# Second accumulator for early maximum units, values through the query/key banks

## What is computed

```python
b, n, _ = x.shape                       # x: layer-normalised, 4 x 1024 x 256, 16 heads of 16
qkv = x @ Wqkv.T + bqkv
q, k, v = ...                           # by head
scores = einsum('bhqd,bhkd->bhqk', q, k) / 4
attn = softmax(scores)
out = einsum('bhqk,bhkd->bhqd', attn, v) -> b, n, 256
return out @ Wo.T + bo
```

## Time and profile before

| | us |
|---|---|
| median of 3 runs | 1923.58 |
| lowest, highest | 1921.22, 1930.8 |
| the profiled execution's own time | 1933.64 |
| its span, first to last instruction | 1931.9 |
| PE busy | 1852.8 (96%) |
| DVE busy | 1354.6 (70%) |
| ACT busy | 1173.1 (61%) |
| the query, key and value phase, first to last product | 635.3 to 769.7 |

### The profile page before, as it was taken

How to read it: one execution, slowest core, us unless ns; L and a number is a source line. 1 busy time by engine, 2 the same in 40 slices (tenths; PEclk the granted TensorE clock), 3 DMA queues, 4 the chain that set the end, 5 groups by cost and what they waited for, 6 DMA issues and landing times. The chain is left out here.

```text
span 1931.9 us, 51788 instructions
## 1 busy us (share of the span) xinstructions
PE 1852.8 (96%) x19838; PEld 1431.7 (74%) x19838; DVE 1354.6 (70%) x2718; ACT 1173.1 (61%) x2355; POOL 432.4 (22%) x509
## 2 busy tenths in 40 slices
PE   7999899999999887999999999999999999999997
PEld 5788789999999644555555555565546789999997
DVE  7566678444436777899999999999944877444445
ACT  4222544444445543898899989989895644445443
POOL 4122001555542322000000000000000002555541
PEclk9999999999999999999999999999999999999999
DMA  7000211222226565321212111111005311222228
GB/s 306 1 1 1 79 45 35 72 77 78 76 68 200 140 171 144 80 52 47 52 47 47 41 42 42 41 42 42 3 3 200 103 36 35 77 75 78 76 68 267
DMA packets 86539, 149.13 MB, mean 77 GB/s; under 512 B 35620, under 2 KB 69284, under 8 KB 80612
## 3 DMA queue, kind: packets, MB, share of 16 engines
q1 hardware_dynamic: 68428, 103.24, 17.8%
q0 software_dynamic: 17856, 42.60, 8.0%
q10 hardware_dynamic: 24, 0.02, 0.0%
HBM read 96.68 MB, written 48.76 MB: 75 GB/s over the span
## 5 line engine op out<-in xcount | busy, mean ns | idle before, releaser
L2212 ACT ACTIVATE att_scores_pt<-att_scores_psE 128x512 f32<-128x512 f32 x1024 | 598.0, 597 | 69.0 <-PE att_scores_psE L1716 26.9
L1731 DVE TENSOR_REDUCE att_mx<-att_scores_psS 128x1 f32<-128x1024 f32 x472 | 577.9, 1224 | 50.1 <-PE att_scores_psS L1716 18.9
L1716 PE MATMUL att_scores_psE<-att_qs,att_ks 99*32 99x512 bf16 x4096 | 437.3, 382 | 4.0 <-DVE att_scores_psO L2242 3.2
L2314 PE MATMUL att_scores_psO<-att_scores_pt,att_va 128*17 128x256 f32 x4096 | 330.4, 379 | 2.9 <-ACT att_scores_osb L2217 1.3
L1716 PE MATMUL att_scores_psS<-att_ks,att_qs 96*32 96x512 bf16 x3776 | 308.4, 380 | 0.1
L1716 PEld LDWEIGHTS att_scores_psE<-att_qs,att_ks 99*32 99x32 bf16 x4096 | 136.0, 95 | 104.0 <-ACT att_scores_pt L2212 8.5
L658 DVE TENSOR_TENSOR moe_hidT_rest<-moe_ps,moe_hidT_high 128x384 fp32r<-128x384 f32 x142 | 79.1, 557 | 184.5 <-ACT moe_hidT_high L377 167.6
L2314 PEld LDWEIGHTS att_scores_psO<-att_scores_pt,att_va 128*17 128x17 f32 x4096 | 131.5, 98 | 103.3 <-issue 13.2
L865 PE MATMUL moe_ps<-W_rest,moe_srcT_high 128*128 (+2 forms) x824 | 200.6, 325 | 0.0
L283 POOL DMA_INDIRECT expert_rows<-work,moe_slots_i x142 | 140.0, 986 | 218.7 <-ACT work L399 101.3
L1716 PEld LDWEIGHTS att_scores_psS<-att_ks,att_qs 96*32 96x32 bf16 x3776 | 126.0, 97 | 78.1 <-issue 1.6
(11 more groups left out here) (325 smaller groups left out, 3154.0 us busy)
## 6 DMA issues: line engine op xcount, KB each, us to landing
W_gate_up<-in_gate_up_dram SPq DMA_DIRECT2D x2, 6346.0 KB, 22.3
work<-expert_rows SPq DMA_DIRECT2D x12, 1024.0 KB, 7.6
query_key_parts<-att_qkv_parts SPq DMA_DIRECT2D x64, 192.0 KB, 3.0
normalised_rows<-work SPq DMA_DIRECT2D x64, 128.0 KB, 1.9
att_qs<-query_key_parts SPq DMA_DIRECT2D x16, 384.0 KB, 4.4
att_ks<-query_key_parts SPq DMA_DIRECT2D x16, 384.0 KB, 4.5
W_down<-in_down_a_dram SPq DMA_DIRECT2D x2, 2304.0 KB, 28.0
work<-normalised_rows SPq DMA_DIRECT2D x36, 128.0 KB, 2.1
```

The costliest lines, as they stand in the source:

```text
L1716: last = nc.tensor.matmul(out[j:j + 32, :], stationary[:, j:j + 32], moving, start=True, stop=True, tile_position=(0, j), skip_group_check ...
L1731: return nc.vector.tensor_reduce(a.mx[g % 2][:, v:v + 1], bank[:, :, :].rearrange("p h k -> p (h k)"), AX.X, ALU.max)
L2212: nc.scalar.activation(pt[s % 2][:, r, :], psE[use % E_BANKS][:, :], ACT.Exp, scale=HD ** -0.5).then_inc(p_ready, 1)
L2314: last = nc.tensor.matmul(psO[32 * r:32 * r + VC, cols], va[g][:, kt, r * VC:(r + 1) * VC], pt[s % 2][:, r, cols], start=(kt == 0 and part ...
```

## The change

Four things are changed in `qkv_phase`.

- psS becomes two buffers of two banks. Units are counted through both groups (n), unit n goes to psS[n % 2] and waits for the reduction of unit n - 2.
- The banks for that come from psV, which now is psQ: value groups 0 and 1 wait for the rests of m = 2 and m = 3, groups 2 and 3 for the copies of 0 and 1, and the next chunk's m = 0 and 1 for the copies of 2 and 3.
- The values are copied to SBUF by ACT (`values_out`), without a bias. The four copies stand at the end of the chunk in ACT's order. DVE loses the four additions, and its xT_rest subtractions come before the second value step instead of the fourth.
- The bias of the values goes into bo, once: it is loaded as two columns, DVE spreads it over 128 columns (Bvb), PE multiplies it with Wo into psB, a part of psS[0], between value groups 1 and 2 of chunk 2, and DVE adds psB to bo.

```diff
-        ps = [ctx.enter_context(nc.psum_tensor(f"{tag}_ps{i}", [P, 512], F32)) for i in range(6)]
-        psT, psQ, psV = ps[0:2], ps[2:4], ps[4:6]
-        psS = ctx.enter_context(nc.psum_tensor(f"{tag}_psS", [P, 2, HALF], F32))
+        ps = [ctx.enter_context(nc.psum_tensor(f"{tag}_ps{i}", [P, 512], F32)) for i in range(4)]
+        psT, psQ, psV = ps[0:2], ps[2:4], ps[2:4]
+        psS = [ctx.enter_context(nc.psum_tensor(f"{tag}_psS{u}", [P, 2, HALF], F32)) for u in range(2)]
+        psB = psS[0][:, 0, 0:D]
...
-            return early[first:first + PER] if c >= BESIDE else []
+            return list(enumerate(early))[first:first + PER] if c >= BESIDE else []
...
+            def values_out(c, j):
+                act.wait_ge(v_done, c * CT + j + 1)
+                nc.scalar.copy(vt[c % 2][j][:, :, 0:HD], psV[j % 2][:, 0:D].rearrange("p (h d) -> p h d", d=HD)).then_inc(v_ready, 1)
...
+                    act.wait_ge(v_stored[c % 2], c // 2 * 16 * CT)
+                elif c == 0:
+                    act.wait_ge(ones_set, 1)
...
                     place_rows(nc.scalar, a, 0, 0)
                 if c + 1 < NCH:
                     rows_out(c + 1)
+                for j in range(CT):
+                    values_out(c, j)
...
-                for g, v in early_maxima(c, i):
-                    dve.wait_ge(a.unit_done, g * UNITS + v + 1)
-                    maximum_reduction(nc, a, psS, g, v).then_inc(a.unit_used, 1)
+                for n, (g, v) in early_maxima(c, i):
+                    dve.wait_ge(a.unit_done, n + 1)
+                    maximum_reduction(nc, a, psS[n % 2], g, v).then_inc(a.unit_used, 1)
...
+            for k in range(KD):
+                last = nc.vector.tensor_copy(bvb[:, k * P:(k + 1) * P], bv[:, k:k + 1].to_broadcast([P, P]))
+            last.then_inc(bv_ready, 1)
...
-                if c >= 2:
-                    dve.wait_ge(v_stored[u], c // 2 * 16 * CT)
...
-                    if c + 1 < NCH and j == CT - 1:
+                    if c + 1 < NCH and j == 1:
                         rows_rest(c + 1)
-                    dve.wait_ge(v_done, c * CT + j + 1)
-                    nc.vector.tensor_tensor(vt[u][j][:, :, 0:HD],
-                                            psV[j % 2][:, 0:D].rearrange("p (h d) -> p h d", d=HD),
-                                            bv[:, :].rearrange("p (h d) -> p h d", d=HD), ALU.add).then_inc(v_ready, 1)
+                    if c == BESIDE - 1 and j == 2:
+                        dve.wait_ge(bo_done, 1)
+                        nc.vector.tensor_tensor(bo[:, :], bo[:, :], psB, ALU.add).then_inc(bo_ready, 1)
...
-                for g, v in early_maxima(c, i):
+                for n, (g, v) in early_maxima(c, i):
                     if v == 0:
                         pe.wait_ge(a.loaded[g], 16 * (LOADS - 1))
-                    if (g, v) != (0, 0):
-                        pe.wait_ge(a.unit_used, g * UNITS + v)
-                    maximum_products(nc, a, psS, g, v).then_inc(a.unit_done, 1)
+                    if n == 0:
+                        pe.wait_ge(bo_ready, 1)
+                    elif n >= 2:
+                        pe.wait_ge(a.unit_used, n - 1)
+                    maximum_products(nc, a, psS[n % 2], g, v).then_inc(a.unit_done, 1)
+
+            def output_bias():
+
+                pe.wait_ge(bv_ready, 1)
+                pe.wait_ge(*wo_loaded)
+                for k in range(KD):
+                    last = nc.tensor.matmul(psB, bvb[:, k * P:(k + 1) * P], wo[:, k, :], start=(k == 0), stop=(k == KD - 1))
+                last.then_inc(bo_done, 1)
...
-                        pe.wait_ge(rest_ready, c * NM + m - 1)
+                        pe.wait_ge(rest_ready, c * NM + m - 1 if m >= 2 else c * NM)
+                    if c and m < 2:
+                        pe.wait_ge(v_ready, c * CT - 1 + m)
...
-                    if c * CT + j >= 2:
+                    if j >= 2:
                         pe.wait_ge(v_ready, c * CT + j - 1)
+                    else:
+                        pe.wait_ge(rest_ready, c * NM + NM - 1 + j)
...
+                    if c == BESIDE - 1 and j == 1:
+                        output_bias()
...
-                sp.dma_start(Bv[:, :], bv.to_broadcast([P, D])).then_inc(attention_loaded, 16)
+                sp.dma_start(Bv[:, :], bv).then_inc(attention_loaded, 16)
...
-        "bv": bqkv[:, 2].reshape(1, D), "bo": att("bo").reshape(1, D),
+        "bv": bqkv[:, 2].reshape(KD, P).T, "bo": att("bo").reshape(1, D),
```

More of the change, by code:

```diff
@@ L1769, in place_rows, with attention_phase @@
         sp.dma_start(a.qs[g][KROWS:MROWS, r, :], a.mxT[g % 2][r * 3:(r + 1) * 3, :]).then_inc(a.mx_rows[g], 16)
-def attention_phase(nc, tag, X, stats, mv, rstd, eps, ident, identb, ones, wqk, wv, wqk_rest, wv_rest, work_at, bqk, bv, bo, wqk_loaded, weights_loaded, qk_d, v_d, O, own_weights):
+def attention_phase(nc, tag, X, stats, mv, rstd, eps, ident, identb, ones, wqk, wv, wqk_rest, wv_rest, work_at, bqk, bv, bvb, bo, wo, wo_loaded, wqk_loaded, weights_loaded, qk_d, v_d, O, own_weights):
     ctx = ExitStack()
@@ L1780, in attention_phase, with qkv_phase @@
         a = HandedOn(sb, sem)
-        qkv_phase(nc, f"{tag}_qkv", X, stats, mv, rstd, eps, ident, identb, ones, wqk, wv, wqk_rest, wv_rest, work_at, bqk, bv, wqk_loaded, weights_loaded, a, qk_d,
+        qkv_phase(nc, f"{tag}_qkv", X, stats, mv, rstd, eps, ident, identb, ones, wqk, wv, wqk_rest, wv_rest, work_at, bqk, bv, bvb, bo, wo, wo_loaded, wqk_loaded, weights_loaded, a, qk_d,
                   v_d, own_weights)
         scores_phase(nc, f"{tag}_scores", X, ident, identb, bo, a, qk_d, v_d, O)
-def qkv_phase(nc, tag, X, stats, mv, rstd, eps, ident, identb, ones, wqk, wv, wqk_rest, wv_rest, work_at, bqk, bv, wqk_loaded, weights_loaded, a, qk_d,
+def qkv_phase(nc, tag, X, stats, mv, rstd, eps, ident, identb, ones, wqk, wv, wqk_rest, wv_rest, work_at, bqk, bv, bvb, bo, wo, wo_loaded, wqk_loaded, weights_loaded, a, qk_d,
               v_d, own_weights):
@@ L1823, in qkv_phase @@
         mid_ready = sem("mid_ready"); lo_ready = sem("lo_ready")
-        v_done = sem("v_done"); v_ready = sem("v_ready")
+        v_done = sem("v_done"); v_ready = sem("v_ready"); bv_ready = sem("bv_ready"); bo_done = sem("bo_done"); bo_ready = sem("bo_ready")
+        ones_set = sem("ones_set")
         parts_stored = [sem(f"parts_stored{u}") for u in range(2)]
@@ L2001, in _ @@
                 for j in range(CT):
-                    nc.vector.memset(vt[u][j][:, :, HD:VC], 1.0)
+                    last = nc.vector.memset(vt[u][j][:, :, HD:VC], 1.0)
+            last.then_inc(ones_set, 1)
             for i in range(KD):
@@ L2556, in memory_moe_attention_moe_kernel @@
             wv_rest = nc.alloc_sbuf_tensor_at("Wv_rest", [P, KD, D], F32R, offset=wv_at)
-            Bqk = alloc(attention, "Bqk", [P, 2 * KD]); Bv = alloc(attention, "Bv", [P, D]); Bo = alloc(attention, "Bo", [P, D])
+            Bqk = alloc(attention, "Bqk", [P, 2 * KD]); Bv = alloc(attention, "Bv", [P, KD]); Bvb = alloc(attention, "Bvb", [P, D]); Bo = alloc(attention, "Bo", [P, D])
             def own_weights(sp):
@@ L2561, in own_weights @@
                 sp.dma_start(Wv[:, :, :], wv).then_inc(attention_loaded, 16)
-                sp.dma_start(Bv[:, :], bv.to_broadcast([P, D])).then_inc(attention_loaded, 16)
+                sp.dma_start(Bv[:, :], bv).then_inc(attention_loaded, 16)
                 sp.dma_start(Bo[:, :], bo.to_broadcast([P, D])).then_inc(attention_loaded, 16)
                 sp.dma_start(Wo[:, :, :], wo).then_inc(wo_loaded, 16)
-            attention_phase(nc, "att", X, stats, mv, rstd, eps, ident, identb, ones, Wqk, Wv, wqk_rest, wv_rest, W["work_at"], Bqk, Bv, Bo, (wqk_loaded, 16), (attention_loaded, 16 * 4),
+            attention_phase(nc, "att", X, stats, mv, rstd, eps, ident, identb, ones, Wqk, Wv, wqk_rest, wv_rest, W["work_at"], Bqk, Bv, Bvb, Bo, Wo, (wo_loaded, 16), (wqk_loaded, 16), (attention_loaded, 16 * 4),
                             qk_d, v_d, work, own_weights)
```

## The result

The changed kernel takes 1910.93 us (median of 6 runs, 1906.31 to 1914.88), the kernel before beside it 1923.99 (6 runs): ratio 0.9934, 95% interval 0.9915 to 0.9953. On a second chip it was 1929.21 against 1936.63: 0.9946 (0.9922 to 0.997). So it is faster, by 13.1 us and by 7.4. The forecast was 1915.8, a gain of 7.8.

What follows compares the result with a forecast made beforehand. PE and DVE taking turns at the single psS was taken as the bound. Gains 7.1 + 3.1 + 1.0 less 0.6, 1.3 and 1.5 made 7.8 us, 1923.58 to 1915.8; range over all cases 1910 to 1922.

Steps and rivals of the forecast that it cites:

- the forecast case: Whole kernel: the summed gain of 7.8 us, time 1915.8, own range 1913 to 1918.5; chance 0.43.
- the rival without a hold: Chunk 7's end: DMA issues do not hold ACT, tail gains 1.9; gain 12.5, time 1911.1; chance 0.15.
- chunks 4 to 6: Second psS removes PE's waits for reductions: 18.29 us per chunk becomes 15.93, gain 7.1.
- chunk 3 from its first unit: Chunk 3, first unit to chunk's end: 17.35 us becomes 14.25, gain 3.1, of it 1.45 from the clock.
- chunk 7 to its last query/key pair: Chunk 7, from its start to that pair: 8.68 us becomes 7.70, gain 1.0.
- first unit later: Chunk 3's first unit starts 0.6 us later (0 to 0.9), as its loads wait behind chunk 1's later stores.
- tail: hold: Chunk 7's end: value copies wait on ACT behind place_rows' four DMA issues; last reduction ends 12.34, not 11.06: -1.3.
- tail: clock: Chunk 7's end: PE stands some 3 us, the clock falls: -1.5 (0.7 to 2).
- the last distance in the slot: From last pair of products to next unit, without a wait: 0.64 us in query/key slots, 0.42 in value slots.
- partial waits: Rival: DVE's uneven load brings back 1 us of wait per chunk; gain 3.8, time 1919.8; chance 0.19.
- the drain: Rival: changing tile shape empties the array for 0.43 us before units, so second psS buys nothing; 1926.3; chance 0.08.
- The chunks before the units: Chunks 0 to 2: third value group waits 1.35 for ACT's copy, next part regains 0.65; 2.1 more on PE.

Runs made afterwards that it cites:

- experiment 1: Changed kernel with all units back in psS[0], each waiting for the reduction just before: 1938.26 us, ratio 1.0015 to the kernel before.
- experiment 3: Changed kernel with each unit as two products of 128 columns instead of eight of 32: 1923.05 us, ratio 0.9921 to the kernel before.
- experiment 4: Changed kernel with the four DMAs of place_rows issued by GpSimd instead of ACT: 1919.47 us, ratio 0.9918 to the kernel before.
- experiment 6: Changed kernel with ACT's copies of value groups 0 and 1 moved earlier, in chunk 7 ahead of place_rows: 1919.25 us, ratio 0.9926 to the kernel before.
- experiment 10: Changed kernel run again without edits, on a second chip: 1929.21 us, ratio 0.9946 to the kernel before.
- experiment 2: Changed kernel with three filler products (six matmuls) in PE's wait before chunk 7's third value group: 1934.14 us, a single run.
- experiment 9: Changed kernel with two-product units, earlier ACT copies, and GpSimd issuing chunk 7's last two part stores and place_rows: 1923.12 us, ratio 0.9927 to the kernel before.

## Why the prediction was right, and where its sum was off

The mechanism is the one forecast: with the second buffer taken back, the chunks are as long as before (experiment 1). 1910.93 lies in the range over all cases, 1910 to 1922, near its lower end, and below the forecast case's own 1913 to 1918.5. By the whole time alone the rival without a hold, at 1911.1, would fit best; the trace shows the hold, so that fit is chance. The sum was 7.8, the stage gained 10.4. By its own terms, forecast and found (us of the stage, result's profile):

| term | forecast | found |
|---|---|---|
| chunks 4 to 6 | 7.1 | 9.4 (54.88 to 45.48) |
| chunk 3 from its first unit | 3.1 | 3.8 (17.35 to 13.58) |
| chunk 7 to its last query/key pair | 1.0 | 1.25 (8.68 to 7.43) |
| first unit later | -0.6 | -1.1 (43.77 to 44.83) |
| tail: hold | -1.3 | -1.0 |
| tail: clock | -1.5 | -2.2 (-1.0 in the repeat) |
| end of the last reduction to the next stage | none | 0.2 |
| sum | 7.8 | 10.4 |

**The slot: the mis-sized term.** The step that failed is the last distance in the slot, taken from "the one place where no wait stands between". The unit at 689.98 did wait. DVE before:

```profile
688.71 1.22 DVE L1731 TENSOR_REDUCE att_mx<-att_qkv_psS 128x1 f32<-128x1024 f32 x1
```

This reduction ends at 689.93. The profile of PE showed no idle because the pair ahead of the unit is modelled as ending at 689.96. That the unit was held shows in its place: of the 39 units behind the first, 37 start 0.05 or 0.06 after the end of the reduction before them, this one too. Without the wait the distance is 0.33. So the 0.42 held 0.09 of the very wait that was to be taken out, and 0.64 was made from it. Eight slots a chunk at 0.09 are 0.7, and 15.93 less that is 15.2; measured is 15.16. Over the 34 slots of the first three rows it is 3.1 of the 3.3 us by which they came out better.

**What does not bound.** Right: one slot of slack was enough, no unit waits, DVE does not come back (partial waits: fallen). All that the narrow shape costs, the drain included, is 0.30 a slot, and it was paid before as well, so it could not cancel the gain (experiment 3).

**The chunks before the units.** Forecast 1.35 lost in the third value group and 0.65 won at the next part, 2.1 over three chunks. Found: chunks 1 and 2 grew by 0.81 and 0.82, chunk 0 by 1.93, 3.6 in all. Part of chunk 0's is its first query/key part at a granted clock of 0.50. The low level began at 627.91, 1.8 us ahead of the stage's first product, while PE stood at the barrier in front of it; what decides between the two levels there was not tried. It costs less than the 1.04 by which the part is longer: in experiments 1, 3 and 4, where the part takes 1.75, chunk 0 lasts 13.86, only 0.7 less than the 14.56 here, since PE then waits 1.5 for DVE's rest. So 2.9 are left for the change, against 2.1 forecast. The order of causes changed with it: the forecast had the loads end last, with 0.5 of idle left; in this profile PE came last, in the repeat the loads (0.88). PE's 2.24 have gone, the clock stayed at 1.00, and chunk 3's second unit is 2.13 behind its first: this part held.

**The bias.** Nothing, as forecast: chunk 2 is no longer than chunk 1, and uncovered it costs 0.64 where 0.8 was the bound (experiment 6). The copies of the values take 0.374 each, by the earlier trace rows 0.37.

**The tail.** The hold is shown: the copies start 0.04 behind the last issue, and with the issues on another engine it is gone (experiment 4). The rule of the Trainium skill quoted with this term (Perfetto Trace Analysis, "DMA Instruction — HWDGE (DVE, Sync)") held. The rival without a hold would have needed a copy at 744.8. The hold's price was 1.0 instead of 1.3: the copy started 0.1 earlier than forecast, and two slots were 0.09 shorter each. The clock cost 2.2 in the result's profile, just over the 2 that was its upper end: the low level lay over both groups and both units, whereas the 1.45 from chunk 3 was one unit and one part. In the repeat it cost 1.0 (experiment 10), so the term holds only as a range.

**The whole time.** What lies between 10.4 and the medians' 13.1 and 7.4 is open; both intervals (9.0 to 16.4 us and 5.8 to 15.1) hold 10.4, and the first leaves out the forecast's 7.8.

## What to carry to other kernels

When two engines take turns at one buffer, the busy shares of both stay below full and the list of waits shows many short ones; here a second buffer gave back the whole wait. Where a bank gets a new reader, look at what stands ahead of that reader in its engine's row, DMA issues too: here two copies at the wrong place cost 5.5 us of the stage (experiment 6), the clock that fell by it included, and the bias nothing. A distance "without a wait" has to be checked against the end of the other engine's work, since a modelled end can hide a wait of a tenth of a microsecond; over 34 slots that was 3.1 us, more than the 2.6 that the whole sum was off by. And where an execution can catch the clock at either level, one profile's sum can agree with another's by luck: compare them term by term.

## What the hardware showed that was not expected

- Units of eight 32-column products between products of 128 columns cost PE 0.09 us going in and 0.20 coming out, against units of two 128-column products (experiment 3). Whether that is the change of shape alone was not separated.
- The same 3.2 or 3.3 us of idle on PE were followed by a granted clock of 0.50 in both profiles of the changed kernel, but in one from 1.5 us before PE went on and in the other from 1.6 us after: 2.2 or 1.0 us of the tail. With six filler products in the wait it stayed at 1.00 (experiment 2, one execution).
- Four DMA issues on ACT's queue held its next instruction for 3.6 us, 0.9 each on the mean; on GpSimd's queue four took 2.19 (experiment 4).
- In experiment 9 the last stores were bounded by the DMA engines, at a share of 1.02 to 1.07 and 275 to 303 GB/s: issuing them 1.5 us earlier, from two queues, did not end the stage sooner.
